# Attention stage and state-space tables: turning normalized rows by DMA transposes instead of TensorE

## What is computed

```python
# state space: 128 channels h, 64 modes n, length 1024
P = dt_Lambda[..., None] * pos - P_max[..., None]
K = jnp.einsum('chn,hnl->chl', Wc, jnp.exp(P)).real
h = concatenate([K, txt], axis=1)                      # (32, 205, 1024)
# attention on layernorm(h)
q, k, v = x @ wq, x @ wk, x @ wv                       # 32, 8, 8 heads of 32
attn = softmax(where(causal, q k^T / sqrt(32), min))
h = h + (attn @ v) @ wo
# linear layer: base weights plus a Fourier-coded low-rank update
h = h + layernorm(h) @ W_eff^T + b_base
```

## Time and profile before

| | |
|---|---|
| runs | 3077.54, 3078.82, 3079.27 us; median 3078.82 |
| profiled execution | 3082.04 us; its span from first to last instruction 3080.3 us |
| TensorE busy | 2781.2 us, 90% of the span; VectorE 65%, ScalarE 36%, GpSimd 33% |
| first matmul of the span | 79.66 us |
| state-space matmuls | 79.66 to 190.7 us |
| attention stage | TensorE from 246.5 to 1890 us |
| whole steps b = 1 to 28 | 397.9 to 1784.2 us |
| output stage | TensorE from 1996 us to the end |
| mean granted TensorE clock | 0.965 |

### The profile page before, as it was taken

The page is one execution under the profiler, slowest core; times in us unless marked ns, Lnnn a source line. Parts: engine busy times, 40 slices in busy tenths (PEclk is TensorE's granted clock), DMA queues, the critical chain, the costliest instruction groups (busy, mean ns, idle before and its releaser), DMA issues. The chain is left out here.

```text
span 3080.3 us, 70678 instructions
## 1 busy us (share of the span) xinstructions
PE 2781.2 (90%) x27970; PEld 2030.8 (66%) x28224; DVE 1997.8 (65%) x4642; ACT 1094.1 (36%) x2362; POOL 1029.9 (33%) x1402
## 2 busy tenths in 40 slices
PE   0847799999999999999999986699999999999999
PEld 0736698989899898989898883244444444444444
DVE  8874577787787878777787865444444444444443
ACT  3331355555555555555555565211001101100110
POOL 4631254544545454554445454011101110110110
PEclk9977899999999999999999996599999999999999
DMA  5642422222222322222222223154554455455453
GB/s 179 194 116 69 103 58 78 58 75 78 57 76 60 80 58 77 69 65 77 56 76 58 69 49 144 55 122 120 129 137 123 121 133 132 118 127 137 124 122 86
DMA packets 446040, 297.32 MB, mean 97 GB/s; under 512 B 389416, under 2 KB 407976, under 8 KB 445232
## 3 DMA queue, kind: packets, MB, share of 16 engines
q1 hardware_dynamic: 445472, 282.69, 35.7%
q10 hardware_dynamic: 240, 10.09, 1.1%
HBM read 116.36 MB, written 80.61 MB: 64 GB/s over the span
## 5 line engine op out<-in xcount | busy, mean ns | idle before, releaser
L693 POOL TENSOR_SCALAR_AFFINE_SELECT p<-p 128x256 f32<-128x256 f32 (+1 forms) x768 | 334.3, 437 | 762.0 <-ACT p L720 743.6
L805 DVE TENSOR_REDUCE mx<-psS 77x2 f32<-77x410 f32 (+1 forms) x768 | 449.3, 613 | 181.9 <-PE psS L912 110.7
L930 PE MATMUL psJ<-xth,qh 128*128 128x205 f16 x2048 | 522.0, 255 | 24.9 <-DVE qsl L813 24.7
L932 PE MATMUL psJ<-xth,ql 128*128 128x205 f16 x2048 | 518.4, 253 | 0.0
L931 PE MATMUL psJ<-xtl,qh 128*128 128x205 f16 x2048 | 516.5, 252 | 0.0
L720 ACT ACTIVATE p<-psT,escale 128x410 f32<-128x410 f32 (+1 forms) x768 | 410.4, 570 | 276.2 <-PE psT L870 256.8
L698 POOL TENSOR_TENSOR pl<-p,ph 128x410 f16<-128x410 f32 (+1 forms) x512 | 447.7, 894 | 102.5 <-ACT ph L727 95.7
L1257 POOL TENSOR_TENSOR hb<-h,bias_sb 128x1024 f32<-128x1024 f32 x52 | 122.5, 2355 | 962.4 <-DVE h L1293 962.4
L1271 ACT CAST xh<-xn 128x1024 f16<-128x1024 f32 x52 | 54.4, 1045 | 967.1 <-DVE xn L1302 967.1
L1332 PE MATMUL ps5O<-woh,ath 128*128 128x512 f16 x832 | 316.2, 380 | 26.3 <-DMA atl<-al 26.3
L1293 DVE SCALAR_TENSOR_TENSOR h<-ps5O,osc,h_in 128x512 f32<-128x512 f32 x104 | 78.1, 751 | 402.4 <-PE ps5O L1334 402.4
(11 more groups left out here) (227 smaller groups left out, 5906.9 us busy)
## 6 DMA issues: line engine op xcount, KB each, us to landing
a_in<-acat SPq DMA_DIRECT2D x52, 512.0 KB, 3.8
h_in<-hcat SPq DMA_DIRECT2D x52, 512.0 KB, 4.7
qst<-qsh SPq DMA_DIRECT2D x512, 51.2 KB, 2.1
out<-y SPq DMA_DIRECT2D x51, 512.0 KB, 3.1
hcat<-ob SPq DMA_DIRECT2D x64, 256.0 KB, 4.0
xin<-hcat SPq DMA_DIRECT2D x32, 512.0 KB
acat<-ao SPq DMA_DIRECT2D x32, 512.0 KB
qst<-qsl SPq DMA_DIRECT2D x256, 51.2 KB, 2.1
```

The costliest lines, as they stand in the source:

```text
L693: pool.affine_select(out=v, in_=v, compare_op=ALU.is_ge, fill=0.0, base=0, pattern=[[0, v.shape[1]], [1, w]], channel_multiplier=-1).then_ ...
L805: dve.tensor_reduce(dst, v, AX.X, ALU.max).then_inc(s_read, 1)
L930: pe.matmul(ps[:, 0:S], wh[:, k, c], xth[:, par, k, :], start=k == 0, stop=False)
L932: m = pe.matmul(ps[:, 0:S], wl[:, k, c], xth[:, par, k, :], start=False, stop=k == KC - 1)
```

## The change

In the attention stage:

- The `x` units and TensorE's 16 transposes a batch are gone. ScalarE subtracts the mean in place (`high_part`, at the end of its slot 3 for the 128 rows and of slot 4 for the 77) and writes the f16 high part `xfh` with the scale of the row; VectorE writes the low part `xfl` in slots 5 and 6 (`low_part`). `layer_norm` in slot 3 now only negates the mean.
- In slot 7 ScalarE issues four DMA transposes (`turn`), after its exponentials and before its casts, from `xfh` and `xfl` into `xth` and `xtl` (128 rows, and 80 rows, of which 3 are padding). TensorE waits for all of them at the start of the next step.
- Loads (slot 2) and stores (slot 2 and slot 6) are issued by ScalarE, no longer by SyncE. A store is one half of the width, since `ao` now holds two halves.
- `norm` takes one reciprocal and one product instead of two and two.

In the state-space stage:

- The sizes come from 36 small ScalarE exponentials whose scale is the step, so the products on GpSimd and one on VectorE go.
- Two fractions instead of four: cosines are taken as sines of a quarter turn less an absolute value.
- All four table products are on VectorE. `SUMMED` goes: each channel has two matmuls.

```diff
@@ ssm
+            act.wait_ge(ab_ok, 1)
+            for k in range(2):
+                for r in range(LR):
+                    m = act.activation(size[:, k, :, r], a[:], ACT.Exp, scale=iqr[:, k, r:r + 1])
+                m.then_inc(size_ok, 1)
...
-            for t in range(4):
-                dve.wait_ge(turned_ok, t + 1)
-                chain(dve.tensor_scalar(tab[:, t], turned[:, t], ROUND, ROUND, ALU.add, ALU.subtract))
-                dve.tensor_tensor(turned[:, t], turned[:, t], tab[:, t], ALU.subtract).then_inc(frac_ok, 1)
+            for k in range(2):
+                m = dve.tensor_tensor(bases[k], per_row(f[:]), per_step(iqr[:, k, :]), ALU.mult)
+            chain(m)
+            chain(dve.tensor_scalar(tab[:, 0], base, phase[:, 0:1], ROUND, ALU.add, ALU.add))
+            dve.scalar_tensor_tensor(turned[:, 0], tab[:, 0], ROUND, base, ALU.subtract,
+                                     ALU.subtract).then_inc(frac_ok, 1)
...
-            for t in (2, 3):
-                dve.wait_ge(sine_ok, t + 1)
-                dve.tensor_tensor(tab[:, t], tab[:, t], size[:, 1], ALU.mult).then_inc(tab_cd, 1)
+            for t in range(4):
+                dve.tensor_tensor(tab[:, t], tab[:, t], size[:, t // 2], ALU.mult).then_inc(tab_ok, 1)
...
-                dve.tensor_tensor(es[:, ch % 2, 0, 0:SUMMED], es[:, ch % 2, 0, 0:SUMMED],
-                                  es[:, ch % 2, 1, 0:SUMMED], ALU.add).then_inc(e_ok, 1)
@@ attention
-                if s >= 4 and has["ln"]:
-                    row.append(("x", s - 4))
...
+            def store(b, half):
+                c = slice(half * D // 2, (half + 1) * D // 2)
+                act.wait_ge(norm_done, 8 * b + 4 * half + 4)
+                act.dma_start(acat[b * S:b * S + P, c], ao[:, half, 0, :]).then_inc(a_out[half], 16)
+                act.dma_start(acat[b * S + P:b * S + S, c], ao[0:TXT, half, 1, :]).then_inc(a_out[half], 16)
+
+            def high_part(b, par, t):
+                r, x = T[t], xin[0:T[t], 1 - par, t, :]
...
+                act.activation(x, x, ACT.Identity, bias=nmean[0:r, t:t + 1]).then_inc(centred, 1)
+                act.wait_ge(centred, 2 * (b + 3) + t + 1)
+                act.activation(xfh[0:r, t, :], x, ACT.Copy, scale=rs[0:r, 3, t:t + 1]).then_inc(x_hi, 1)
+
+            def turn(t, to, n):
+                r, cols = ((P, slice(0, P)), (TROWS, slice(P, P + TROWS)))[t]
+                act.wait_ge(x_hi, 2 * n + t + 1)
+                act.dma_start_transpose(out=xth[:, to, :, cols], in_=xfh[0:r, t, :]).then_inc(xt_in[to], 16)
+                act.wait_ge(x_lo, 2 * n + t + 1)
+                act.dma_start_transpose(out=xtl[:, to, :, cols], in_=xfl[0:r, t, :]).then_inc(xt_in[to], 16)
...
+                    if g == 2 and has["load"]:
+                        wait(act, x_lo, 2 * (b + 3))
+                        load(b + 4, par)
+                    if g == 2 and has["last"]:
+                        store(b - 1, 1)
+                    if g == 6 and has["att"]:
+                        store(b, 0)
...
+                    if g == NKV - 1 and has["ln"]:
+                        wait(act, pj_filled, base)
+                        for t in range(2):
+                            turn(t, 1 - par, b + 3)
...
+                    if g in (3, 4) and has["ln"]:
+                        high_part(b, par, g - 3)
...
+                elif g == 3:
+                    dve.tensor_scalar(nmean[:], mv[:, :, 0], -1.0, None, ALU.mult).then_inc(ln_done, 1)
+
+            def low_part(b, par, t):
+                r = T[t]
+                dve.wait_ge(x_hi, 2 * (b + 3) + t + 1)
+                dve.scalar_tensor_tensor(xfl[0:r, t, :], xin[0:r, 1 - par, t, :], rs[0:r, 3, t:t + 1], xfh[0:r, t, :],
+                                         ALU.mult, ALU.subtract).then_inc(x_lo, 1)
...
+                if has["qkv"]:
+                    pe.wait_ge(xt_in[par], 64 * ((b + 2) // 2 + 1))
                 for g in SLOTS:
```

More of the change, by code:

```diff
@@ L183, in _ @@
                       allow_small_or_imprecise_dtypes=True).then_inc(iota_ok, 1)
[L184 to L191, removed]
             pool.wait_ge(gg_ok, 1)
             pool.wait_ge(in_x, 32)
-            pool.wait_ge(frac_ok, 4)
+            pool.wait_ge(frac_ok, 2)
             for ch in range(NCH):
@@ L205, in _ @@
             act.activation(dt[:], ldt[:], ACT.Exp).then_inc(dt_ok, 1)
+            act.wait_ge(ab_ok, 1)
[3 more added lines that the diff above has]
+                m.then_inc(size_ok, 1)
+            for la in range(LA):
+                m = act.activation(ela[:, la, :], a[:], ACT.Exp, scale=ila[:, la:la + 1])
+            m.then_inc(la_exp_ok, 1)
             act.wait_ge(args_ok, 1)
@@ L376, in _ @@
                         pe.wait_ge(k_read, n - 3)
-                    last = 0 if j < SUMMED else 1
-                    for k in range(last + 1):
+                    for k in range(2):
                         m = pe.matmul(ps[n % 4][:, j % 2, :], u[:, ch % 2, j].rearrange("p a c -> p (a c)"),
-                                      es[:, ch % 2, k, j, :], start=k == 0, stop=k == last)
+                                      es[:, ch % 2, k, j, :], start=k == 0, stop=k == 1)
                     if j % 2:
@@ L613, in step @@
                     shift_rows(1, par)
-                if has["load"]:
-                    wait(sp, pj_filled, base)
-                    load(b + 4, par)
                 if b == -1:
@@ L621, in step @@
                         sp.dma_start(dst, src).then_inc(arrived, 16)
-                if has["last"]:
-                    store(b - 1, nxt)
                 if has["qkv"]:
@@ L746, in norm @@
                 n = 8 * b + g
-                if g == 0:
-                    wait(dve, a_out[par], 16 * (b - par))
+                if g % 4 == 0:
+                    wait(dve, a_out[g // 4], 32 * b)
                 dve.wait_ge(av_done, n + 1)
@@ L838, in step @@
                         layer_norm(b, par, g)
+                    if has["ln"] and g in (5, 6):
+                        low_part(b, par, g - 5)
                     if has["att"] and g:
@@ L947, in unit @@
                     m = pe.transpose(ps[0:NH // 2, P:S], mx[0:TXT, 1, heads], ident[0:TXT, 0:TXT])
-                else:
-                    t, half = divmod(n, 2)
-                    pe.wait_ge(ln_done, 2 * (b + 4))
-                    r = T[t]
-                    for k in range(4):
-                        c = 4 * half + k
-                        m = pe.transpose(ps[:, k * r:(k + 1) * r], xin[0:r, 1 - par, t, c * P:(c + 1) * P], ident[0:r, 0:r])
                 if last:
```

135 lines of the change are left out of this document (65 added, 70 removed).

## The result

The changed kernel takes **3324.18 us** (median of 4 runs, 3322.74 to 3331.42), the kernel before 3079.05 beside it (3077.54 to 3081.98): a ratio of 1.080, 95% interval 1.0781 to 1.0818. The forecast was 3213, with a range up to 3315. The sign came out as forecast, and so did most waits. The size did not: +245 us, not +134, just outside the range.

What follows compares the result with a forecast made beforehand. TensorE, busy 90% of the span, was taken as the bound. Per-step terms summed to +4.9 us, times 29 +142; with -18, +8 and +2 outside, 3082 became 3216, or 3213 us as median, range 3105 to 3315.

Steps and rivals of the forecast that it cites:

- Rival (1): Step start: transposes fight with the K copies, a wait of 6.6 us, +4.8 a step, 3352 us; chance 0.17.
- my own case: Whole kernel: 3213 us, from 3150 (no clock lost, passes at their lower bound) to 3290; chance 0.60.
- Rival (2): Slot 7: ScalarE posts transposes like plain copies, the wait is 1.3 us, no clock lost, 3106 us; chance 0.11.
- The wait for four transposes: Start of each step: TensorE idles +3.4 us until the fourth transpose lands, 7.9 us into slot 7.
- ScalarE's two passes: Slots 4 and 5: passes delay exponentials, +1.0 us each, +2.0 a step (bounds 1.0 and 2.6); VectorE no bound.
- Clock: Slot 0: TensorE loses granted clock after the 3.4 us stall, +1.6 us a step (bounds 0 and 3.2).
- Loads ahead of slot 2: Slot 2: loads and stores ahead of ScalarE's exponentials delay the third score matmul, +0.6 us a step.
- Fewer kst waits: Steady steps: TensorE's waits for K's restacked rows go, -0.35 us a step (bounds 0 and -0.35).
- Turning leaves TensorE: Slots 4 to 7: turning rows no longer takes TensorE's time, waits included, -2.31 us a step.
- "-18" for the state-space stage: Before the first matmul: shorter VectorE preparation, net -18 us (bounds -12 and -24).
- "+8" for the start of attention: Start of attention: memsets, loads, ScalarE's passes, issues and landing replace TensorE's turning, +8 us (bounds 4 and 13).
- "+2" for the last steps: Last steps: stores ahead of exponentials cost +2 us.

Runs made afterwards that it cites:

- spread: The change, with the four transposes issued one at a time, three of them ahead of the third exponentials of slots 5 to 7: 3160.33 us, ratio 1.0238.
- vec_norm: The change, with VectorE normalizing in slot 3 as before, one ScalarE pass a tile and a plain subtraction for the low part: 3228.18 us, ratio 1.0472.
- sp_copies: The change, with loads and stores issued by SyncE again instead of ScalarE: 3318.62 us, ratio 1.076.
- ssm_k_first: The kernel before, with the change's state-space stage and K's rows copied ahead of Q's: 3055.13 us, ratio 0.9928.
- change_k_first: The change, with the one edit that K's rows are copied ahead of Q's: 3312.74 us, ratio 1.0761.
- short: The change, with the two transposes of 80 rows left out from step -1 on, to price an issue: 3225.91 us, ratio 1.0479.
- k_first_gaps: The change with one ScalarE pass, transposes spread over slots 4 to 7, K's rows first, loads and stores in gaps, later TensorE wait: 3019.35 us, ratio 0.9812.
- k_first: The change with one ScalarE pass, one transpose in each of slots 4 to 7, and K's rows copied ahead of Q's: 3041.37 us, ratio 0.9878.

## Why the prediction was right or wrong

**Right in kind.** The stall at each step's start released by the DMA into `xtl`, the lost clock behind it, the late exponentials of slots 2, 4 and 5, the nearly unchanged slot 3 (7.44 against 7.60), K's waits gone, the earlier first matmul: each stands in the trace. The experiments took most of the stall (spread), the delays of slots 4 and 5 (vec_norm), that of slot 2 (sp_copies) and K's waits (ssm_k_first) away one at a time. Rival (1), with a stall of 6.6 us and 3352, was nearer than my own case, but not for its reason: other neighbours change nothing (change_k_first).

Rival (2), cheap posting, falls by one row. On the same queue a plain copy is held 0.35 us, a transpose 1.30 to 1.45:

```profile
L690 ACTq DMA_DIRECT2D xin<-hcat x32: 332/346/357, 217.9 to 1926.0; - x32
```

The Trainium skill's page "Advanced Engine Details and Errata", section X-Bar Transpose (TRN2), has transposing DMAs as fast as regular ones. Taken for what an issue costs the engine that makes it, that does not hold in this trace.

**Wrong in size**, by 3.7 us a step (58.12 against 54.4), which over 28 steps is 103 of the 111 us that were missing:

- *The wait for four transposes*, "+3.4": the step that failed. It ended 10.34 us into slot 7, not 7.88, 2.5 more. "For the pieces of 80 rows I take 0.8, in proportion" is 1.0 of that: an issue of 80 rows holds the queue 1.30 us (short). Landing took 1.7 after the last issue, not 1.2: 0.5. The first issue took 1.44, not 1.24: 0.2. Most of the rest, some 0.5 on average, is that in about every second step one of the four took 1.9 to 2.9.
- *ScalarE's two passes*, "+2.0", and "VectorE is no bound here": slots 4 to 6 came out at 16.55 together, not 15.7. With one pass on ScalarE and a plain subtraction on VectorE they take 13.56, so the change's passes cost 3.0 against that, above my bound of 2.6. Of that 0.56 is slot 6, where VectorE's low pass of 1.99 us makes the maxima late. I had counted VectorE's passes and not where they stand.
- *Clock*, "+1.6": slot 0 is 9.58 against 7.30, so +2.3. The bounds 0 and 3.2 held it. The loss does not grow with the stall within the change: slot 0 takes 9.75 behind the 13 stalls of 4.7 to 4.8 us, 9.44 behind the 15 of 5.0 to 6.4.
- *Loads ahead of slot 2*, "+0.6": +0.5. *Fewer kst waits*, "-0.35": exactly that. *Turning leaves TensorE*, "-2.31": in step 29 of the changed kernel slots 4 to 7 take 18.0, where a full step took 20.5 before, so -2.5; 0.2 of it has another cause, since step 29 of the kernel before, which turns nothing, takes 18.2.
- *The range of my own case*, "from 3150 (no clock lost, passes at their lower bound)", is added up wrongly: 29 times 1.6 and 29 times 1.0 less than 3213 is 3138.

**Outside the steps.** "-18" for the state-space stage: -16.5 at the first matmul, -15 at the last, -15.4 alone. "+8" for the start of attention: the first projection starts at 243.87 instead of 250.86, 7 earlier, so +8. "+2" for the last steps: -1 (1295.1 us behind step 28, 1296.1 before).

**Where the time went**, on the whole: in each step a stall of 5.3 us, 2.3 of clock behind it, 3.0 for the order of ScalarE's and VectorE's passes, 0.5 for the loads, against some 2.5 that TensorE saved. The cost lies in where the issues and passes stand, not in turning by DMA at all: with the issues in idle time, one pass less, K's copies first and the loads and stores in gaps the same idea gives 3019 us, 36 less than turning on TensorE with the same state-space stage and order of copies.

**What stays open.** Why one issue in every second step is long. In the trace of the change all 15 issues above 1.8 us have a packet of the instruction queue (16 KB) within the microsecond before them or under them, and the longest issue without one is 1.49 us; but 13 issues with such a packet nearby were not long, and one long issue in vec_norm, one in k_first_gaps and two in k_first have no such packet. No run changes it. That VectorE's low pass in slot 4 makes slot 5 take 5.70 in the fastest kernel is read from its rows; no run moves the pass.

## What to carry to other kernels

When work moves to another engine's queue, price the issues, not the bytes, and ask what TensorE waits for at the end of that queue: four issues in a row behind the last exponential were a stall, one at a time in gaps of a microsecond they were free. A pass that is cheap in busy time can still be dear by its place, and the engine that receives it (here VectorE, 57% busy) has an order too. After a stall is removed look for what it hid, before adding anything to the next queue.

## What the runs showed of the hardware

- A DMA transpose on ScalarE's queue holds it 1.27 to 1.49 us in 113 of the change's 128 issues, with a median of 1.45 and 1.37 us for the two of 128 rows of 1024 f16, and 1.30 for both of 80; a plain copy on the same queue 0.35.
- VectorE's `scalar_tensor_tensor` over 1024 columns took 1.98 to 2.03 us in the steady steps, beside GpSimd's subtractions, and 1.27 to 1.28 in the first three batches, where GpSimd has no work of this stage. The plain subtraction took 1.21 to 1.23 in those batches, and 1.22 or 2.02 beside GpSimd. In the kernel before, L298 took 2.29 us alone and 6.48 beside GpSimd's products of L191. The Trainium skill's page "Vector Engine (DVE) Microarchitecture Reference", section Points that are easy to get wrong, says that this form with two sources that are not bf16 halves throughput. The 1.27 us of the first batches, with the same sources, speak against that as a general rule.
- In spread, stalls of 0.42 to 1.39 us left the next slot at a granted clock of 1.00, those of 1.58 to 2.47 us at 0.81; in the change, one of 4.76 us left it at 0.73.
- ScalarE issues a DMA before the instruction ahead of it has begun: in k_first_gaps the issue at 1088.93 us stands behind an exponential that starts at 1089.24.
